# Routed recurrent layer: the passage from routing to experts, with one tile's x instead of two taken from the input

## What is computed

```python
xn = layernorm(x)                                  # x: (4, 2048, 512), float32
h_t = h_{t-1} * A + xn_t                           # recurrence along the 2048 positions
s = h @ BC                                         # 512 x 512
e = argmax(xn @ gate_w.T)                          # one of 8 experts for each token
g = silu(xn + xn @ expert_w[e].T)                  # 512 x 512 for each expert
out = x + s * g
```

## Time and profile before

| | |
|---|---|
| median of 3 runs | 513.97 us (513.12 to 515.68) |
| the profiled execution, its time | 516.85 us |
| its span, first to last instruction | 515.1 us |
| TensorE busy | 494.1 us (96%) |
| VectorE, GpSimd, ScalarE busy | 407.5, 330.1, 260.4 us |
| mean granted clock of TensorE, as a share of full speed | 0.987 |

### The profile page before, as it was taken

How to read it: one execution, slowest core, us unless ns; L and a number is a source line. 1 busy time by engine, 2 the same in 40 slices (tenths; PEclk the granted TensorE clock), 3 DMA queues, 4 the chain that set the end, 5 groups by cost and what they waited for, 6 DMA issues and landing times. The chain is left out here.

```text
span 515.1 us, 10789 instructions
## 1 busy us (share of the span) xinstructions
PE 494.1 (96%) x2722; PEld 387.2 (75%) x2723; DVE 407.5 (79%) x1076; ACT 260.4 (51%) x500; POOL 330.1 (64%) x394
## 2 busy tenths in 40 slices
PE   7999999999999999999977999999999999999993
PEld 6667777777777777777655878887888888888782
DVE  4999999999899999999833777776778777767773
ACT  4676776776687677677431333333333333333330
POOL 2467667766776766765763666667766666656652
PEclk9999999999999999999989999999999999999997
DMA  8979778787877877874447577777777776767620
GB/s 244 356 229 276 225 256 254 241 242 241 264 226 240 276 220 247 264 230 166 149 116 242 184 241 233 239 221 237 240 234 229 245 237 210 229 184 240 218 83 9
DMA packets 65667, 114.80 MB, mean 223 GB/s; under 512 B 9994, under 2 KB 28042, under 8 KB 65632
## 3 DMA queue, kind: packets, MB, share of 16 engines
q1 hardware_dynamic: 47328, 62.46, 38.7%
q0 software_dynamic: 18304, 51.99, 32.0%
HBM read 66.48 MB, written 55.08 MB: 236 GB/s over the span
## 5 line engine op out<-in xcount | busy, mean ns | idle before, releaser
L1135 PE MATMUL ps_s<-w_hi,split 128*128 x284 | 118.9, 419 | 2.8 <-DVE split L930 2.6
L526 POOL DMA_INDIRECT out_dram<-work x71 | 75.0, 1057 | 64.2 <-issue 38.3
L682 ACT ACTIVATE ps_s<-ps_s 128x512 f32<-128x512 f32 x71 | 41.3, 582 | 147.2 <-PE ps_s L1137 106.0
L1136 PE MATMUL ps_s<-w_lo,split 128*128 x284 | 112.8, 397 | 0.0
L1137 PE MATMUL ps_s<-w_hi,split 128*128 x284 | 112.7, 397 | 0.0
L423 POOL TENSOR_TENSOR split<-work,split 128x1024 fp32r<-128x1024 f32 x31 | 74.7, 2411 | 47.7 <-ACT split L589 47.7
L1030 PE MATMUL ps_s<-bc_hi,split 128*128 128x512 f32 x256 | 104.2, 407 | 0.6 <-ACT split L589 0.5
L1031 PE MATMUL ps_s<-bc_lo,split 128*128 128x512 f32 x256 | 101.2, 395 | 0.0
L508 POOL DMA_INDIRECT work<-token_rows,work x68 | 73.1, 1076 | 26.3 <-issue 22.4
L441 POOL DMA_INDIRECT slot_table<-token_id,slot_id x64 | 64.6, 1010 | 29.6 <-issue 25.9
L727 DVE TENSOR_TENSOR_SCAN work<-a_col,work,ps_xt 128x256 f32<-128x256 f32 x112 | 74.3, 722 | 0.0
(11 more groups left out here) (125 smaller groups left out, 739.7 us busy)
## 6 DMA issues: line engine op xcount, KB each, us to landing
token_rows<-work SPq DMA_DIRECT2D x31, 528.0 KB, 3.2
work<-in_L_attn_inputs_dram SPq DMA_DIRECT2D x31, 512.0 KB
token_rows<-work SPq DMA_DIRECT2D x29, 512.0 KB
work<-in_L_ffn_expert_w_dram SPq DMA_DIRECT2D x128, 64.0 KB
slot_table<-w_lo SPq DMA_DIRECT2D x1, 2080.0 KB, 12.7
token_rows<-in_L_attn_inputs_dram SPq DMA_DIRECT2D x3, 512.0 KB, 10.5
out_dram<-work POOLq DMA_INDIRECT x71
work<-token_rows,work POOLq DMA_INDIRECT x68
```

The costliest lines, as they stand in the source:

```text
L526: nc.gpsimd.indirect_dma_start(out=out_flat, out_offset=bass.IndirectOffsetOnAxis(ap=slot_tok[:, n:n + 1], axis=0), in_=o_sb[:, u], in_off ...
L1135: nc.tensor.matmul(z_ps[v], hi, wh, start=(k == 0), stop=False)
L1136: nc.tensor.matmul(z_ps[v], hi, wl, start=False, stop=False)
```

## The change

`FIRST` becomes 1 (one tile's slots from the plan, one `first_ids`), `SPLIT` becomes 1 (only tile 0's x by `gather_head`), and `MID` = 3 takes the place of `FIRST` for the tiles whose successor is turned within `expert`. The rest moves steps:

```diff
@@ constants
-    FIRST = 3
-    SPLIT = 2
+    FIRST = 1
+    MID = 3
+    SPLIT = 1
...
-        HEAD = (RR - 1, RR - 3)
+        HEAD = (RR - 1,)
@@ GpSimd
             count(0, TAIL)
+            next_ids(0, TAIL + 1)
+            add_identity(0, TAIL + 1)
             scatter_ids(0, TAIL)
-            low_part(0, TAIL + 1)
             count(0, TAIL + 1)
-            next_ids(0, TAIL + 1)
+            next_ids(0, TAIL + 2)
             scatter_ids(0, TAIL + 1)
-            next_ids(0, TAIL + 2)
             scatter_ids(0, TAIL + 2)
-            add_identity(0, TAIL + 1)
             add_identity(0, TAIL + 2)
...
             first_ids(0)
-            first_ids(1)
+            all_ids()
             gather_head(0)
-            first_ids(2)
-            gather_head(1)
-            all_ids()
             for v in range(2):
                 pool.wait_ge(s_stored[v], 16 * (GROUPS // 2 + (TPG - 1 if v == LAST else 0)))
+            gather(0, 1)
             gather(0, 0)
             gather(0, 2)
-            gather(0, 1)
@@ ScalarE
             high_part(0, TAIL + 2)
             take_mv(0, TAIL + 1)
+            block_high(0, TAIL + 1)
             take_mv(0, TAIL + 2)
             for t in range(TPG):
                 take_half(0, TAIL + 1, t)
-            block_high(0, TAIL + 1)
+            take_half(0, TAIL + 2, 0)
             block_high(0, TAIL + 2)
-            for t in range(TPG):
-                take_half(0, TAIL + 2, t)
+            take_half(0, TAIL + 2, 1)
@@ VectorE
-            scan(0, TAIL + 1)
+            scan(0, TAIL + 1, between=True)
             block_low(0, TAIL - 1)
             turn_w(TAIL)
-            route(0, TAIL + 1, False)
+            route(0, TAIL + 1, False, behind=False)
             scan(0, TAIL + 2, between=True)
+            block_low(0, TAIL)
             route(0, TAIL + 2, False, behind=False)
...
                                            ALU.add).then_inc(slot2_ready, 1)
+            turn_w(TAIL + 1)
             step(nc.vector.tensor_scalar(done[:, :], tile_cum[:, :], j_col[:, 0:1], None, ALU.is_le), 9)
...
             nc.vector.tensor_tensor(blk_row[:, :], pick[:, 2:3], pick[:, 1:2], ALU.subtract).then_inc(blk_row_ready, 1)
+            for c in range(TAIL + 1, GROUPS):
+                dve.wait_ge(hi_done, c + 1)
+                dve.wait_ge(lo_done, c)
+                nc.vector.tensor_tensor(hs_lo[c % 2], hs[:, c % 2], hs_hi[c % 2], ALU.subtract).then_inc(lo_done, 1)
+            block_low(0, TAIL + 1)
+            turn_w(TAIL + 2)
...
             nc.vector.tensor_scalar(e_row[:, :], e_row_f[:, :], float(E - 1), None, ALU.min).then_inc(e_row_ready, 1)
-            dve.wait_ge(hi_done, GROUPS)
-            dve.wait_ge(lo_done, GROUPS - 1)
-            nc.vector.tensor_tensor(hs_lo[LAST], hs[:, LAST], hs_hi[LAST], ALU.subtract).then_inc(lo_done, 1)
-            for c in range(TAIL, GROUPS):
-                block_low(0, c)
-                if c + 1 < GROUPS:
-                    turn_w(c + 1)
+            block_low(0, TAIL + 2)
...
+            dve.wait_ge(blk_loaded, 16)
+            nc.vector.tensor_copy(blk_f[0:PLANNED], blk_i[0:PLANNED, :, 0]).then_inc(blk_f_ready, 1)
+            dve.wait_ge(slot_turned, 1)
+            nc.vector.tensor_copy(slot_tok[:, :], slot_ps[:, 0:TILES]).then_inc(slot_tok_ready, 1)
             normalise(0, 0)
             low_x2(0, 0)
-            dve.wait_ge(blk_loaded, 16)
-            nc.vector.tensor_copy(blk_f[0:PLANNED], blk_i[0:PLANNED, :, 0]).then_inc(blk_f_ready, 1)
             normalise(0, 1)
-            dve.wait_ge(slot_turned, 1)
-            nc.vector.tensor_copy(slot_tok[:, :], slot_ps[:, 0:TILES]).then_inc(slot_tok_ready, 1)
             low_x2(0, 1)
             normalise(0, 2)
@@ TensorE
-            score_parts(0, b)
+            score_parts(0, b, placed=True)
...
             product_hi(0, b, 1, part=range(1, CH))
+            product_hi(0, c, 0)
+            product_hi(0, c, 1)
             product_lo(0, b, 0)
             product_lo(0, b, 1)
-            product_hi(0, c, 0)
-            product_hi(0, c, 1)
             product_lo(0, c, 0)
             product_lo(0, c, 1)
...
-            stay_busy(18)
+            stay_busy(13)
...
-                    if isinstance(it, int) and it + c < FIRST and k == CH - 3:
+                    if isinstance(it, int) and it + c < MID and k == CH - 3:
                         turn_x2(0, c + 1)
-                    if isinstance(it, int) and it + c == 0 and k == CH - 2:
-                        turn_slots()
...
             pe.wait_ge(w_lo_done, BLOCKS)
+            turn_slots()
+            stay_busy(5)
             turn_x2(0, 0)
             stay_busy(6)
             for c in range(RR):
-                tile(0, c, ahead=c >= FIRST)
+                tile(0, c, ahead=c >= MID)
```

## The result

The changed kernel took 511.57 us in the median of six runs, from 510.04 to 512.68, against 514.18 for the kernel before beside it: a ratio of 0.9922, with an interval of 0.9893 to 0.9951. A second series (the first experiment) gave 0.9945, 0.9911 to 0.9979. So it is faster by some 0.5 to 0.8%, 3 to 4 us, where 5.5 us (508.5) were forecast and 505.2 to 511.3 was the range. The median itself is 0.3 us above that range; put on the 513.97 us from which the forecast was made, the first ratio gives 510.0 and the second 511.1, both inside it. The profiled execution took 511.46 us with a span of 509.7, 5.4 us less than the span of before. That is more than the runs gained, and explaining it turned out to be half of the work.

What follows compares the result with a forecast made beforehand. TensorE, full in the tile phase, bounds the kernel, so only the passage between the halves can give: 4.5 (tile 0's start) + 1.2 (clock) + 2.6 (old idles) - 3.0 (new stalls) = 5.5 us, rounded; 513.97 to 508.5, range 505.2 to 511.3.

Steps and rivals of the forecast that it cites:

- the two old idles: TensorE's waits in the kernel before, 0.28 us ahead of tile 1 and 2.33 ahead of tile 2; 2.6 us of gain.
- the second rival: The port, or a late landing: line reads 0.8 to 2.4 us late delay tile 0's x; gain 2.6 to 4; chance 0.15.
- the signs of being wrong: `product_lo(30)` waits, TensorE idles over 1 us ahead of the slots, the clock falls, or later tiles' period exceeds 3.27.
- the passage: Stretch between the kernel's halves, measured from the first filler to tile 3's slot in TensorE's queue; 19.7 us forecast.
- The passage should be as long in both: Profiled execution (516.85 us) and median (513.97) were taken to have equal passages, so 513.97 - 5.5 = 508.5.
- The landings: DMA times from issue to arrival: block 3.1 us, tile 0's x 3.1, last store of s 3.2.
- The held issue: VectorE's low parts may hold GpSimd's issues, on top of `add_identity(31)` and `first_ids(0)`; taken as 0, upper bound 2.4 us.
- Rows 0, 2 and 3 at 2.0 each: Full-row gathers after tile 1's were to follow at some 2.0 us each, giving stalls of 0.6 and 0.9.
- the port: Port pair shared by VectorE and GpSimd as exclusive lock; GpSimd up to 2.4 us later; in a rival of chance 0.15.
- the third: Rival: block or x over 2 us late, tile 0 again at 1.2 GHz; gain 0 to 2.6; chance 0.08.

Runs made afterwards that it cites:

- the first experiment: The changed kernel again with no edit, in more rounds beside the kernel before; ratio 0.9945 (0.9911 to 0.9979).
- the low part early: Changed kernel with group 30's low part made between group 31's scans and routing, and group 30's products first again; ratio 0.9944 to the kernel before.
- the mended one: Low part early plus two tiles' x from the input, block right behind the first line read, tile 1's x in buffer 1; 0.9873 to the kernel before, 508.04 us.
- the tail alone: Changed kernel with only the last groups' new order kept, everything from the reads of lines on as in the kernel before; ratio 0.9960 to that kernel.

## Why the prediction was right, and where its sizes were off

The direction, the place and the mechanism held: the tile phase starts earlier and stays full, the scatters and the first read come 3.8 us earlier (3.5 forecast), and the two old idles give way to waits for the rows of tile 1 (1.32 us in both profiles) and of tile 2 or 3 (0.40, 0.72). The size didn't: 5.5 was forecast, 4 to 7 as its bounds, and the runs gave 2.6 us between medians in the first series, 4.0 by its ratio and 2.8 by that of the second. That is the gain of the second rival (2.6 to 4); the stated range held because it took that rival in. Two of the signs of being wrong came up faintly, `product_lo(30)` with its 0.3 us, inside the bound of 0.5, and 0.99 and 1.09 us idle ahead of the slots where 1 was the limit. What is missing between 5.5 us and the gain in the passage has two nearly equal parts, the first two below.

- **"The passage should be as long in both"** is the step that failed. The profiled execution was 2.9 us over the median, and I explained that away. It had the clock fall in the passage (1.2 us of gain were even counted for it); the two later profiles of the same kernel had not, and their passage was 23.8 instead of 25.2. So 1.4 us of the forecast gain exist only in a part of the executions. How large that part is, the mean clocks suggest: 14 of 28 runs of the kernel before have 0.988 or less, and of the 18 of the changed kernel in the two series none (0.991 to 0.997).
- **The landings** were taken from rows with fewer bytes beside them. Block 4.06 instead of 3.1, x 4.1 instead of 3.1, and 4.3 for the last store of s, for which 3.2 was the median row: its last half was issued at 260.0 and let GpSimd go at about 264.3, where 263.4 was forecast. The first gather, that waits for it and for the token numbers (263.8), left at 265.39, 1.1 after GpSimd's queue had begun on it; 0.88 was taken for that. I had seen the 1.06 MB and allowed 0.5 us for them; with block and x they fill the rings for 5 us. The passage was 20.8 to 21.35 instead of 19.7.
- The held issue, taken at 0 with a bound of 2.4, measured 0.9 (1.93 instead of 1.05); four stretched instructions and one that began first and wasn't speak for a lock that the first to start holds. The Trainium skill, page "SBUF — State Buffer", in its list on where engines contend, has just this: whichever of the two starts first gets the pair for the whole instruction. By that rule the bound would have been the rest of the one low part under way, not the length of both, and the trace agrees: the second low part ended at 256.58, 0.99 after the read began. It put tile 0's x later, not tile 1's row, so it cost less than its 0.9.
- Rows 0, 2 and 3 at 2.0 each were 1.8 to 1.9 (tile 1's x used at 269.88, tile 2's at 273.44, tile 3's at 275.32): in the changed kernel tile 2 idled 0.40 and not 0.9.
- Of the rivals the second is nearest to what came, in its size; of its two causes the port did come, for 0.9 us, but what was late most wasn't the read of lines, it was the block and x behind it. The price of the third, a slow clock in tile 0, was wrong: while tile 1 waits for its row, it costs nothing (no fillers, 0.9932). It costs where TensorE is what everything waits for, as in the kernel before.

What is open: why the last store of s still held GpSimd until 263.7 with the low part early, some 4 us after its last half was issued, when the rings had room (share 0.75 in 261 to 263, 0.03 in 263 to 265). The same two halves landed after 2.4 and 2.2 us in the two later profiles of the kernel before, 4.3 in the changed kernel, and 2.9 in the mended one. It wasn't taken apart further; the mended kernel goes round it.

## What to carry to other kernels

Before a sum is made against a profile, look at whether that execution is a typical one, above all at its granted clock; a profile 0.6% over the median has its excess somewhere, and it may sit in the very stretch that the change is about. Where a change makes several transfers due at once, add their bytes and divide by the rate that the windows show with full rings (277 to 387 GB/s in the changed kernel's windows with a share of 0.98 or more, 330 over the passage's 5 us), and don't take each one's latency alone. And where a row waits for a store, ask what needs the row: here only x was urgent, and fetching it from the input for two tiles, into buffers that nothing else wants soon, with the block ahead of the second read and group 30's low part early, was worth 2.5 us or more of the passage.

## What the hardware showed that I had not expected

The clock's fall doesn't follow from the length of one idle stretch: 3.58 us idle left it at 1.00 in one execution of the kernel before, 3.36 us was followed by 0.50 in another, and so was 2.24 us in the kernel with the low part early and 1.81 us in that with the tail alone. And taking 13 fillers away lowered the clock to 1.2 GHz for over 6 us at no cost that the runs can tell.
